# One transformer block with a mixture of experts: the epsilon of two layer norms as an operand in PSUM, a GpSimd subtraction in halves around a power, two tiles normalised on ScalarE, sums per group

## What is computed

```
h = tokenise(x)                                # 896 x 128
h = h + LN(attn(LN(h)) + LN(h)) * gamma + beta # attention over 14 positions, 8 heads
f = LN(h)                                      # eps 1e-5
y = sum over the best 2 of 10 experts of gate * (elu(f W1 + b1) W2 + b2)
s = conv1(silu(conv9(f)))                      # the shared branch
h = h + LN(f + y + s) * ln_g + ln_b
router logits = conv3(gelu(conv3(f)))
```

## Time and profile before

| | us |
|---|---|
| median of 3 runs | 169.5 |
| lowest, highest | 168.96, 170.34 |
| the profiled execution, its own time | 169.95 |
| its span | 168.1 |

### The profile page before, as it was taken

The page is one execution under the profiler, slowest core; times in us unless marked ns, Lnnn a source line. Parts: engine busy times, 40 slices in busy tenths (PEclk is TensorE's granted clock), DMA queues, the critical chain, the costliest instruction groups (busy, mean ns, idle before and its releaser), DMA issues.

```text
span 168.1 us, 3081 instructions
## 1 busy us (share of the span) xinstructions
PE 156.6 (93%) x1020; PEld 137.7 (82%) x1020; DVE 131.8 (78%) x351; ACT 78.1 (46%) x192; POOL 86.0 (51%) x75
## 2 busy tenths in 40 slices
PE   7998899999999999989995999999999999999870
PEld 2887689899965648879994997999999999989730
DVE  0087999979999999879971558798989998893492
ACT  2222857211045639951031333777777888741040
POOL 1052799999998592003777600054545545442040
PEclk9999999999999999999999699999999999999999
DMA  5999999966940000000397159939889995100604
GB/s 164 287 409 394 231 187 230 211 82 117 187 70 2 0 0 6 0 0 0 70 312 282 48 123 318 403 146 324 276 318 283 334 319 188 47 31 20 218 0 109
DMA packets 19698, 28.35 MB, mean 169 GB/s; under 512 B 4983, under 2 KB 14338, under 8 KB 19683
## 3 DMA queue, kind: packets, MB, share of 16 engines
q1 hardware_dynamic: 17062, 21.47, 42.7%
q0 software_dynamic: 1696, 5.52, 13.9%
q10 hardware_dynamic: 924, 1.17, 2.4%
HBM read 19.73 MB, written 5.28 MB: 149 GB/s over the span
## 4 chain that ended last, share of the span: by engine, by line
PE 63%; DVE 21%; issue 5%; DMA 4%; ACT 2%; POOL 1%; SPq 0%; DVEq 0%; POOLq 0%
PE psum L703 15%; PE psum L743 13%; PE psum L731 11%; PE psum L613 6%; PE psum L545 4%; PE psum L514 3%; DVE stats L1129 2%; DMA wring<-ys_rows 2%; DVE psum L1196 2%; DVE prod L360 2%; DVE veps L1135 2%; DMA ys_rows<-yb,xid 2%; PE psum L525 2%; PE psum L539 2%; DVE mv L1132 1%
## 5 line engine op out<-in xcount | busy, mean ns | idle before, releaser
L499 POOL DMA_INDIRECT ys_rows<-yb,xid x22 | 21.6, 981 | 30.1 <-ACT yb L1086 28.3
L1076 ACT ACTIVATE wu<-psum,wring 128x128 f32<-128x128 f32 x92 | 26.1, 372 | 9.1 <-PE psum L731 7.2
L1390 DVE SCALAR_TENSOR_TENSOR tb<-psum,wring,wu 128x128 f32<-128x128 f32 x92 | 25.9, 344 | 0.8
L743 PE MATMUL psum<-wring,tb 128*128 128x128 f32 x184 | 25.0, 279 | 0.2
L731 PE MATMUL psum<-xTb,wring 128*128 128x128 f32 x184 | 24.3, 275 | 0.0
L489 POOL DMA_INDIRECT xs_rows<-xT_s,slot x14 | 14.1, 1008 | 18.1 <-DVE slot L1321 14.1
L743 PEld LDWEIGHTS psum<-wring,tb 128*128 128x128 f32 x184 | 22.3, 191 | 1.2 <-issue 0.6
L731 PEld LDWEIGHTS psum<-xTb,wring 128*128 128x128 f32 x184 | 22.4, 192 | 0.5 <-issue 0.5
L613 PE MATMUL psum<-prod,ident_s 128*128 128x196 f32 (+1 forms) x120 | 21.6, 341 | 0.0
L613 PEld LDWEIGHTS psum<-prod,ident_s 128*128 128x128 f32 x120 | 21.1, 190 | 0.0
L360 POOL TENSOR_TENSOR prod<-es,vt 128x3136 f32<-128x3136 f32 x3 | 18.9, 6319 | 0.0
(11 more groups left out here) (178 smaller groups left out, 279.0 us busy)
## 6 DMA issues: line engine op xcount, KB each, us to landing
wring<-wexp SPq DMA_DIRECT2D x23, 514.0 KB, 4.7
wu<-raw POOLq DMA_DIRECT2D x2, 1536.0 KB, 11.7
raw<-wsh SPq DMA_DIRECT2D x2, 768.0 KB, 8.5
xs_rows<-zero_s SPq DMA_DIRECT2D x1, 1472.0 KB, 16.6
ys_rows<-zero_s SPq DMA_DIRECT2D x1, 896.0 KB, 18.9
xT_s<-xT SPq DMA_DIRECT2D x2, 384.0 KB, 5.5
wu<-wsh SPq DMA_DIRECT2D x1, 768.0 KB, 6.6
xb<-xs_rows SPq DMA_DIRECT2D x1, 585.0 KB, 6.7
```

Of the source, the lines that this page charges most:

```text
L499: pool.indirect_dma_start(ys_dram, bass.IndirectOffsetOnAxis(ap=xid[:, j:j + 1], axis=0), yb[:, j % NY, :], None)\
L743: ins = mm(ps[Y_BANK][:, 0:D], tb[:, j % NTT, c, :], wring[:, j % NR, W2 + c * P:W2 + (c + 1) * P], start=(c == 0), stop=(c == HC - 1))
L1076: ins = A(eb[:, j % NEB, c, :], ps[U_BANKS[j % NU]][:, c * P:(c + 1) * P], ACT.Exp, bias=wring[:, j % NR, B1 + c:B1 + c + 1])
L1390: ins = V.scalar_tensor_tensor(tb[:, j % NTT, c, :], ps[U_BANKS[j % NU]][:, c * P:(c + 1) * P], wring[:, j % NR, B1 + c:B1 + c + 1], eb[:, ...
```

## The change

- L1135: for norms 1 and 2 the epsilon is no longer an immediate number of a `tensor_scalar` whose input and output are in SBUF. It is a second tensor, written once into a free corner of PSUM (bank 6, columns 256 to 262), and the addition is a `tensor_tensor` of that and of the variance. The `memset` that writes it, and a wait for it, stand on VectorE ahead of norm 1's first statistics.
- GpSimd: the second of the two L477 subtractions is cut in halves of 128x768. `inv_std(1, 0)` stands between the halves; the other powers stand behind the second half. The semaphore `wu_l_pool` is counted to 3 in place of 2.
- TensorE: residual, bias and products follow each other group by group. The products with no use behind them are 7 in place of 12.
- ScalarE: the second copy of a weight (L985) comes after the seven diagonals in place of ahead of them. ScalarE normalises tiles 3 and 4 of `x3` (two new instructions, signal `x3_act`), with scale 1/std and bias -mean/std.
- VectorE: computes -mean/std of these two tiles (one `scalar_tensor_tensor` of 128x2, both inputs in SBUF, signal `nmr_done`), after a wait for `rstd_done` of group 1, and normalises the five tiles that remain.

```diff
--- before.py
+++ after.py
@@ -79,8 +79,8 @@
 K_PLACE = [(5, 0), (7, 0), (1, 0), (2, 256)]
 V_BANK = (5, 7)
 XT_BANK = 3
-FILL = (11, 12, 1, 4)
-IDLE_BANK = 0
+FILL = (11, 7, 1, 4)
+IDLE_BANK, EPS_BANK, EPS_COL = 0, 6, 256
 
 HW = N // 2
 FHALVES = [(0, HW), (HW, N)]
@@ -473,11 +473,17 @@
             pool.wait_ge(S("rch_done"), 1)
             pool.tensor_tensor(wrc1_l[:], wrc1_s[:], wrc1_h[:], ALU.subtract).then_inc(S("rc_split"), 1)
             pool.wait_ge(S("wu_h_done"), 2)
-            for k, m in enumerate((0, 3)):
-                pool.tensor_tensor(wu03_l[:, k], raw02[:, k], wu_h[:, m], ALU.subtract).then_inc(S("wu_l_pool"), 1)
-            for n in (1, 2):
-                for k in range(len(GROUPS)):
-                    inv_std(n, k)
+            pool.tensor_tensor(wu03_l[:, 0], raw02[:, 0], wu_h[:, 0], ALU.subtract).then_inc(S("wu_l_pool"), 1)
+            outer = [t.rearrange("p g n -> p (g n)") for t in (wu03_l[:, 1], raw02[:, 1], wu_h[:, 3])]
+            for k in range(2):
+                part = slice(k * 3 * DHID // 2, (k + 1) * 3 * DHID // 2)
+                pool.tensor_tensor(*(t[:, part] for t in outer), ALU.subtract).then_inc(S("wu_l_pool"), 1)
+                if k == 0:
+                    inv_std(1, 0)
+            for k in (1, 2):
+                inv_std(1, k)
+            for k in range(len(GROUPS)):
+                inv_std(2, k)
             pool.wait_ge(S("wu_h_done"), 3)
             pool.tensor_tensor(wu12_l[:, 0], wu12[:, 0], wu_h[:, 1], ALU.subtract).then_inc(S("wu1_l"), 1)
             pool.wait_ge(S("xs_zero"), 32)
@@ -528,8 +534,11 @@
 
             def x3_transposes(k):
 
-                for i in LN_GROUPS[k]:
-                    pe.wait_ge(S("x3_done"), i + 1)
+                for n, i in enumerate(LN_GROUPS[k]):
+                    if k == 1:
+                        pe.wait_ge(S("x3_act"), n + 1)
+                    else:
+                        pe.wait_ge(S("x3_done"), (k // 2) * len(LN_GROUPS[0]) + n + 1)
                     col = (i - LN_GROUPS[k][0]) * P
                     ins = nc.tensor.transpose(ps[X3_BANKS[k]][:, col:col + P], x3[:, i, :], ident_s[:])
                 ins.then_inc(S("x3T_mm"), 1)
@@ -668,7 +677,6 @@
             for bank, tiles in zip(H2_BANKS, LN_GROUPS):
                 residual(bank, h, tiles)
                 bias_row(4, ps[bank][:, 0:len(tiles) * D], tiles, False)
-            for tiles in LN_GROUPS:
                 for i in tiles:
                     pe.wait_ge(S("scaled_mean"), i + 1)
                     pe.wait_ge(S("diag_done"), i + 1)
@@ -776,7 +784,7 @@
             def low_weights(c, m, last=True):
 
                 if m in (0, 3):
-                    pe.wait_ge(S("wu_l_pool"), 2)
+                    pe.wait_ge(S("wu_l_pool"), 3)
                 else:
                     pe.wait_ge(S(f"wu{m}_l"), 1)
                 product(c, m, 2, last)
@@ -982,18 +990,21 @@
             act.wait_ge(S("wu_sum"), 32)
             A(wu_h[:, 1], wu12[:, 0], ACT.Copy).then_inc(S("wu_h_done"), 1)
             context_rows(1)
-            A(wu_h[:, 2], wu12[:, 1], ACT.Copy).then_inc(S("wu_h_done"), 1)
 
             for k, tiles in enumerate(LN_GROUPS):
                 act.wait_ge(S("rstd_done"), ln_count(1, k))
                 for i in tiles:
                     A(xnT[:, i * P:(i + 1) * P], ident_s[:], ACT.Identity, bias=cols_s[:, C_ZERO:C_ZERO + 1], scale=rstd[:, 1, i:i + 1])\
                         .then_inc(S("diag_done"), 1)
+            A(wu_h[:, 2], wu12[:, 1], ACT.Copy).then_inc(S("wu_h_done"), 1)
+            act.wait_ge(S("nmr_done"), 1)
+            for i in LN_GROUPS[1]:
+                A(x3_t[i], h2_ps[i], ACT.Identity, bias=nmr[:, 2, i:i + 1], scale=rstd[:, 2, i:i + 1]).then_inc(S("x3_act"), 1)
             for k in range(len(LN_GROUPS)):
                 act.wait_ge(S("x3T_mm"), k + 1)
                 A(by_tile(xh[:])[:, tile_range(2, k)], tile_columns(k), ACT.Copy).then_inc(S("xh_done"), 1)
 
-            act.wait_ge(S("wu_l_pool"), 2)
+            act.wait_ge(S("wu_l_pool"), 3)
             for k in range(len(LN_GROUPS)):
                 act.wait_ge(S("xl_done"), k + 1)
                 A(xp[:, 2:T + 2].rearrange("p (h i) b -> p i h b", h=2)[:, tile_range(2, k)], tile_columns(k), ACT.Copy)\
@@ -1132,7 +1143,11 @@
                     ins = V.bn_aggr(mv[:, n, i, :], stats[:, n, i, :])
                 link(ins)
                 sl = tile_range(n, hf)
-                V.tensor_scalar(veps[:, n, sl], mv[:, n, sl, 1], EPS, None, ALU.add).then_inc(S("var_done"), 1)
+                if n in (1, 2):
+                    ins = V.tensor_tensor(veps[:, n, sl], ps[EPS_BANK][:, EPS_COL:][:, sl], mv[:, n, sl, 1], ALU.add)
+                else:
+                    ins = V.tensor_scalar(veps[:, n, sl], mv[:, n, sl, 1], EPS, None, ALU.add)
+                ins.then_inc(S("var_done"), 1)
 
             def normalise(k):
 
@@ -1237,6 +1252,8 @@
             V.memset(rT9[:, 0, 0, :], 0.0).then_inc(S("zeroed"), 1)
             V.memset(rT9[:, NT + 1, 1, :], 0.0).then_inc(S("zeroed"), 1)
             V.memset(both[:, NT, :], 0.0).then_inc(S("zeroed"), 1)
+            V.memset(ps[EPS_BANK][:, EPS_COL:EPS_COL + NT], EPS).then_inc(S("zeroed"), 1)
+            dve.wait_ge(S("zeroed"), 4)
             dve.wait_ge(S("o_mm"), 1)
             ln_stats(1, o_ps, 0)
             scaled_less_mean(0)
@@ -1248,9 +1265,12 @@
             for k, tiles in enumerate(LN_GROUPS):
                 dve.wait_ge(S("h2_mm"), tiles[-1] + 1)
                 ln_stats(2, h2_ps, k)
-            for k in range(len(LN_GROUPS)):
+            dve.wait_ge(S("rstd_done"), ln_count(2, 1))
+            sl = tile_range(2, 1)
+            V.scalar_tensor_tensor(nmr[:, 2, sl], mv[:, 2, sl, 0], -1.0, rstd[:, 2, sl], ALU.mult, ALU.mult).then_inc(S("nmr_done"), 1)
+            for k in (0, 2):
                 normalise(k)
-            dve.wait_ge(S("wu_l_pool"), 2)
+            dve.wait_ge(S("wu_l_pool"), 3)
             for a in (0, T + 2):
                 V.memset(xp[:, a:a + 2], 0.0).then_inc(S("xp_zero"), 1)
             for k in range(len(LN_GROUPS)):
```

## The result

The changed kernel has a median of 168.13 us over 13 runs (167.3 to 169.37), the kernel before 169.22 over its 13 (168.73 to 170.34). The ratio is 0.994, with a 95% interval of 0.9915 to 0.9965.

The account below looks back on a forecast made before the run. VectorE's own list was taken to bound the kernel from 50 us; gains of 0.86 up to the last statistics and 0.44 in normalising, less 0.05 for `form`, sum to -1.25 us: median 168.25 us, range 166.9 to 169.6.

Parts of the forecast that it names:

- next statistics: VectorE's statistics after its wait for the Wo products: to start at 52.83 instead of 54.04, 1.21 us earlier.
- last statistics start: VectorE's norm 2 statistics of group 2, behind TensorE's products: to start at 58.0, gain so far 0.86 us.
- `xl` done: VectorE's `xl` after the transposes and ScalarE's copies: to end at 62.1 instead of 63.41, a gain of 1.3 us.
- product with `dsf_l`: TensorE's first product with `dsf_l`, behind the changed part: to start at 66.65 instead of 67.89 us.
- The stretch: From the end of VectorE's last `ctx_s` to TensorE's first product with `dsf_l`: forecast 1.25 us shorter.
- group 2's wait for its products: VectorE waits for TensorE's group 2 residual and products before the last statistics: 0.35 of the 1.21 us lost again.
- the stall of 2.18 us: VectorE's L1135 stood until GpSimd's subtraction ended; freeing it brings the following statistics 1.21 us earlier, not 1.84.
- The copy's move: ScalarE's L985 (1.48 us) would be in the way of the power ending at 52.5, so it goes behind.
- `form` behind L482: VectorE's `form`, two SBUF inputs, may be blocked by GpSimd's last subtraction L482: price 0.05 us (0 to 0.3).
- Rival B: VectorE's -mean/std gets behind GpSimd's L482 and waits until 63.17: +4.1 us, total 172.4; chance 0.05.
- Rival D: Five fewer filling products drop TensorE to half clock before the router convolution: up to 2 us more, 170 to 171; chance 0.04.
- Rival C: TensorE's stall at 90 us and slow clock behind it, 3.6 us in all, vanish: 164.7 us; chance 0.07.

Follow-up runs that it names:

- e9b: Changed kernel with GpSimd's second subtraction in three parts (704, 512, 320 elements) instead of halves: stretch 16.30 us, ratio 0.9928 to the kernel before.
- e8: Changed kernel with -mean/std waiting for the last group's power, so it becomes ready as GpSimd's long subtraction starts: stretch 21.42 us, time 173.83 us.
- e5: Changed kernel with all seven tiles normalised on VectorE, without -mean/std and ScalarE's two tiles: stretch 16.94 us.
- e12b: Changed kernel with 12 filling products in place of 7: stretch 17.04 us.
- e7: Changed kernel with all residuals and biases ahead of the products again: stretch 17.27 us.
- e1: Kernel before with only the epsilon moved to PSUM: stretch 17.63 us, ratio 0.9988.
- e4: Kernel before with epsilon in PSUM, the halves and the order by groups: stretch 17.39 us, ratio 0.9977.
- e6: Changed kernel with epsilon as an immediate number again: stretch 17.35 us, with GpSimd entering late.
- e10b: Changed kernel unaltered, run once more beside others on one chip: stretch 16.57 us, ratio 0.9916 to the kernel before.

## Why the prediction was right

By its steps, times from the cut (prediction, measured in the changed kernel):

| step | predicted | measured |
|---|---|---|
| addition of epsilon | 0.18 | 0.16 |
| first power ends | 2.5 | 2.52 |
| a half subtraction | 1.76 | 1.77, 1.78 |
| next statistics | 2.81 | 2.82 |
| second, third power end | 4.93, 5.63 | 4.95, 5.60 |
| last statistics start | 8.0 | 7.90 |
| `xl` done | 12.1 | 12.06 |
| product with `dsf_l` | 16.6 | 16.54 |

The stretch was forecast at -1.25 and is -1.33. The one term that is off by more than the reading is group 2's wait for its products, 0.35 forecast, 0.25 measured.

The total came closer than the sum earned, and that part is luck. I took 1.25 off a median of 169.5 and got 168.25; the measured 168.13 stands beside 169.22, the kernel before in more runs, a difference of 1.09. In the profiled pair the 1.4 us are 0.70 from the start and 1.33 from the stretch, less 0.60 in the tail: two terms that my sum did not have and that nearly cancel.

That the stall of 2.18 us would give 1.2 and not 1.84 on VectorE, and that GpSimd's second half and group 2's residual would take part of it back, was the step that mattered. The experiments make it sharper than I had it. Epsilon, halves or both give 0.22 to 0.24; only with the order by groups does VectorE's advance reach norm 2. Taken out of the finished kernel, the order by groups costs 0.73, the fewer filling products 0.50, ScalarE's tiles 0.40, and epsilon 0.81 as measured or some 0.46 with GpSimd on time. The sum is 2.44, or 2.1, though the whole is 1.33: each part guards the same path, so neither the additions one by one nor the removals one by one add up. The halves were not taken out of the finished kernel, so what they are worth in it is not shown; e9b shows only that three parts gain 0.24 over two. The copy's move, which I argued was needed, is the part that does nothing: I compared its end with the power it precedes, and not with the slack of the products behind it, though I had worked that slack out.

`form` behind L482 was given 0.05 and cost nothing that can be seen. Rival B (0.05) is shown as a mechanism by e8 and has its margin: its power ended at 57.81 and the subtraction began at 58.93. Rival D is not seen at 7 products: the granted clock stayed whole until 90 us.

Rival C, the stall at 90 us, goes with the chip here, not with the kernel. In the changed kernel it is there as before, a gap of 1.97 us and then two windows of 2 us at 0.66 and 0.50 of the clock, shifted with the rest:

```profile
...
90.00:92.00 2.00, 2.00 (x9) 1.94 (x8) 0.00 (x0) 1.43 (x2) 1.39 (x3) 0.66 0.13 44
92.00:94.00 2.00, 2.00 (x8) 1.92 (x7) 1.96 (x6) 0.00 (x0) 1.70 (x2) 0.50 0.21 67
...
```

The gap is there in all profiles of e5 to e12b (1.92 to 2.14, in e7 1.27). In the four of e1 to e4, all on one chip, TensorE has no gap over 0.10 between 80 and 100 us, the clock stays at 1.00, and the middle takes 33.0 us instead of 36.1 to 36.8:

```profile
...
90.00:92.00 2.00, 2.00 (x13) 1.95 (x12) 1.93 (x6) 0.00 (x0) 1.62 (x2) 1.00 0.28 98
...
```

The kernel before took 165.0 us there, in one session, and 169.2 to 169.9 elsewhere. What makes it is open, and the 3.6 us that I had for it are right in size and wrong in their parts. I had 2 us of gap and 1.6 of slow clock. But in e6, e7, e10b and e12b the clock does not fall behind the gap, and the middle is no shorter: 36.42, 36.11, 36.69 and 36.75. TensorE waits again instead, in e6 for 0.63 and 0.36 us. So the fall of the clock adds nothing that the middle shows. What fits the 3.5 us is how late ScalarE is, some 3.4. Its copy of the gates starts 0.5 us behind the first of TensorE's seven transposes in e1 (87.19, 86.66) and 3.9 behind it in the kernel before (91.13, 87.19), and TensorE later waits for that copy.

## What to carry to other kernels

Cut both traces at an instruction ahead of the change and at one behind it, and compare the distances: here that resolved 0.03 us where the whole span varies by more than the gain. Then check where each of the other engines stands at the first cut: in two of 14 profiles GpSimd was 0.35 us late, which reads like an effect of the edit and is none. A stall at the head of a hand-over between engines is worth only what the next wait leaves of it, so list for each engine when it would be ready and when it is wanted, and take the latest; parts that guard one path have to be put in together. An instruction of two numbers can stand for a whole long one on GpSimd: look at where its inputs lie, not at its size.

## What the runs showed of the hardware

- VectorE beside a GpSimd subtraction with both inputs in SBUF: an addition of a number, SBUF to SBUF, stood until its end (2.18, 0.57, 0.85, 0.92, 1.27 us in place of 0.17); a `scalar_tensor_tensor` with two inputs in SBUF too (3.37 in place of 0.15, e8); a `tensor_tensor` with one input in PSUM not (0.16). The Trainium skill (SBUF — State Buffer, "Who interferes with whom") states all three, and the trace agrees.
- On one chip the kernel before ran 4.2 to 4.9 us faster than in the other sessions (165.0 against 169.2 to 169.9), and some 3.5 us of it lie in the middle, with the stall at 90 us (33.0 in e1 to e4, on that chip, against 36.1 to 36.8).
- After 4 us in which TensorE idled (e8), its clock was granted 0.69 and 0.50 in the two windows from 64 us on. Behind the gap of about 2 us near 90 us it fell in some profiles (0.66 and 0.50 in the changed kernel's) and stayed at 1.00 in others (e6, e10b, e12b); the changed kernel itself shows both, in its first profile and in e10b.
